# Output stores of the last stage split over two DMA queues, even token tiles on ScalarE's and odd ones on SyncE's

## The reference

```python
logits = jnp.einsum('ed,btd->bte', gate_w, x)
scores = jax.nn.sigmoid(logits) + gate_b
weights, indices = jax.lax.top_k(scores, TOP_K)          # TOP_K = 4
weights = weights / weights.sum(-1, keepdims=True)
...
h3 = jax.nn.silu(h1 * h2)                                # per expert
experts_out = jnp.einsum('btec,ecd->bted', h3, w2_routed)
routed_out = jnp.einsum('bted,bte->btd', experts_out, router_probs)
return shared_out + routed_out
...
x = x + jnp.tanh(g_ffn[0]) * _L0_ffn_ref(_layernorm(x), ...)
```

## Time and profile before

| what | us |
|---|---|
| median of 3 runs | 913.25 (912.56 to 913.78) |
| the profiled execution | 911.14 |
| its span, first to last instruction | 909.4 |
| TensorE busy | 787.8 (87%) |
| GpSimd busy | 505.7 (56%) |
| VectorE busy | 453.4 (50%) |
| ScalarE busy | 285.7 (31%) |

### The profile page before, as it was taken

The page is one execution under the profiler, slowest core; times in us unless marked ns, Lnnn a source line. Parts: engine busy times, 40 slices in busy tenths (PEclk is TensorE's granted clock), DMA queues, the critical chain, the costliest instruction groups (busy, mean ns, idle before and its releaser), DMA issues.

```text
span 909.4 us, 16740 instructions
## 1 busy us (share of the span) xinstructions
PE 787.8 (87%) x4484; PEld 684.9 (75%) x4485; DVE 453.4 (50%) x916; ACT 285.7 (31%) x572; POOL 505.7 (56%) x361
## 2 busy tenths in 40 slices
PE   4455869888995979999999999998899999999991
PEld 3233667666774869998998998997789998888891
DVE  5886868897867553334333333333233333333331
ACT  1426537456351112222222222222132232222220
POOL 1744075083278670250786751776870587978782
PEclk9776969998998979999999999999899999999997
DMA  7448176189133433352566454464552469779999
GB/s 256 152 134 287 47 286 240 56 318 388 38 153 111 183 111 101 93 166 70 153 188 179 147 150 127 142 196 130 162 188 81 126 191 197 164 164 210 215 188 266
DMA packets 68858, 153.54 MB, mean 169 GB/s; under 512 B 6720, under 2 KB 8768, under 8 KB 68832
## 3 DMA queue, kind: packets, MB, share of 16 engines
q0 software_dynamic: 24400, 70.86, 30.0%
q1 hardware_dynamic: 33920, 61.13, 20.7%
q10 hardware_dynamic: 10512, 21.23, 6.4%
HBM read 85.43 MB, written 67.76 MB: 168 GB/s over the span
## 4 chain that ended last, share of the span: by engine, by line
PE 59%; DVE 12%; POOL 12%; DMA 4%; ACT 4%; issue 4%; ACTq 2%; POOLq 0%; SPq 0%; DVEq 0%
PE bank L600 32%; PE bank L617 14%; POOL ring_lo L436 4%; DMA wa<-in_ctx_dram 3%; PE bank L1013 3%; PE bank L608 3%; POOL acc L570 3%; PE bank L625 2%; PE bank L710 2%; POOL dispatched L474 2%; DVE amax L1454 2%; POOL ring_hi L434 2%; PE bank L728 1%; ACTq L1163 1%; DVE xa L1447 1%
## 5 line engine op out<-in xcount | busy, mean ns | idle before, releaser
L600 PE MATMUL bank<-ring_hi,xr_hi 128*128 x632 | 170.4, 351 | 16.3 <-DVE xr_lo L1917 16.3
L600 PE MATMUL bank<-ring_lo,xr_hi 128*128 x632 | 156.2, 329 | 0.0
L600 PE MATMUL bank<-ring_hi,xr_lo 128*128 x632 | 155.8, 328 | 0.0
L434 POOL CAST ring_hi<-raw 128x1408 fp32r<-128x1408 f32 x34 | 47.0, 1382 | 169.6 <-PE bank L600 158.6
L600 PEld LDWEIGHTS bank<-ring_hi,xr_hi 128*128 128x128 f32 x632 | 107.1, 193 | 40.3 <-issue 40.2
L1069 ACT ACTIVATE ht_hi<-bank 128x384 fp32r<-128x384 f32 x95 | 46.7, 492 | 281.1 <-PE bank L608 281.1
L1926 DVE TENSOR_TENSOR ht_lo<-bank,ht_hi 128x384 fp32r<-128x384 f32 x79 | 44.1, 558 | 170.7 <-ACT ht_hi L1069 170.6
L617 PE MATMUL bank<-ring_hi,ht_hi 112*128 (+3 forms) x285 | 120.4, 422 | 3.6 <-DVE ht_lo L1926 1.3
L600 PEld LDWEIGHTS bank<-ring_lo,xr_hi 128*128 128x128 f32 x632 | 113.6, 192 | 0.0
L600 PEld LDWEIGHTS bank<-ring_hi,xr_lo 128*128 128x128 f32 x632 | 113.5, 192 | 0.0
L570 POOL DMA_INDIRECT acc<-expert_out,out_row x64 | 99.6, 1556 | 24.7 <-issue 24.7
(11 more groups left out here) (181 smaller groups left out, 1295.9 us busy)
## 6 DMA issues: line engine op xcount, KB each, us to landing
raw<-in_L_ffn_w_routed_dram POOLq DMA_DIRECT2D x32, 704.0 KB, 4.9
x_in<-dispatched SPq DMA_DIRECT2D x79, 264.0 KB, 2.9
expert_out<-zero_rows ACTq DMA_DIRECT2D x9, 2304.0 KB, 19.2
expert_out<-y_out SPq DMA_DIRECT2D x79, 256.0 KB, 2.9
raw<-in_L_ffn_w_routed_dram POOLq DMA_DIRECT2D x16, 448.0 KB
dispatched<-zero_rows SPq DMA_DIRECT2D x1, 4224.0 KB, 27.6
acc<-in_x_dram SPq DMA_DIRECT2D x4, 1024.0 KB, 11.4
wa<-in_fside_BxS2xS_dram SPq DMA_DIRECT2D x4, 1024.0 KB, 6.7
```

Of the source, the lines that this page charges most:

```text
L434: g.tensor_copy(hi, raw13[:, :, m, :]).then_inc(s[rounded], 1)
L600: last = mm(outs[m], half[:, c * P:(c + 1) * P], ring13(w, slot_at, c, m), start=(c == 0 and half is x_hi and w is ring13_hi), stop=(c == ...
```

## The change

The 16 output stores are divided. ScalarE's queue gets those of the even token tiles, behind its last `tile_step`; SyncE keeps those of the odd ones. Each still waits for the four gathers of its own token tile. SyncE's two waits for the stores to `expert_out` stand behind its output stores now, and not ahead of them. SyncE's last wait, for all 16 output stores, is unchanged.

```diff
                 sp.wait_ge(s["d_y_e"], t + 1)
                 store_tile(t, t % 2)
 
+            for t in range(1, TT, 2):
+                sp.wait_ge(tile_gathered[t], 16 * TOPK)
+                sp.dma_start(out_rows[t], acc_tile(t)).then_inc(s["out_stored"], 16)
             for k in range(2):
                 sp.wait_ge(y_stored[k], 16 * ((TILES + 1 - k) // 2))
-            for t in range(TT):
-                sp.wait_ge(tile_gathered[t], 16 * TOPK)
-                sp.dma_start(out_rows[t], acc_tile(t)).then_inc(s["out_stored"], 16)
             sp.wait_ge(s["out_stored"], 16 * TT)
...
             for t in range(3 + 2 * len(range(3, TILES - 2, 2)), TILES + 1):
                 tile_step(t, t % 2)
+            for t in range(0, TT, 2):
+                act.wait_ge(tile_gathered[t], 16 * TOPK)
+                act.dma_start(out_rows[t], acc_tile(t)).then_inc(s["out_stored"], 16)
```

## The result

| kernel | median us (runs) | ratio to before, 95% interval |
|---|---|---|
| before | 912.86 (6, 909.95 to 913.78) | |
| with the change | 908.19 (6, 907.13 to 911.21) | 0.9959 (0.994 to 0.9978) |

The kernel is faster by 0.41%, some 3.7 us, with an interval from 2.0 to 5.5 us. I had forecast 0.24% and 911.05 us, with a range down to 910.3.

What follows compares the result with a forecast made beforehand. The prediction took DMA work with one hole to bound the last 20 us. Gains of 1.70 us (hole) and 0.5 us (rate), less 0 for late gathers, made 2.2 us: 913.25 to 911.05 us, range 910.3 to 912.7.

Steps and rivals of the forecast that it cites:

- What bounds the end: Last 20 us: DMA work sets the end, with one hole while SyncE waits for the last expert store.
- first term: Stretches from 895 us: earlier output stores fill the hole in DMA work, gaining 1.70 us (1.0 to 1.75).
- second term: Output stores at the end: two queues write at 411 GB/s instead of 382, gaining 0.5 us (0 to 0.78).
- third term: Last gathers sharing engines with stores: tile 15's lands later, at about 901, costing 0 us (0 to 1.7).
- rivals of late: Tile 15's gather lands at 904 to 905, leaving a new hole; gain 0 to 1.3 us; chance 0.18.
- dearer gathers: Gathers mixed with stores cost more per packet, so DMA work grows and the time is over 915 us; chance 0.06.
- The level and the range: Median 913.25 us less 2.2 gives 911.05; lower end 910.3 allows 0.4 us for run-to-run movement, upper end 912.7.

Runs made afterwards that it cites:

- SyncE alone: Against the kernel before, all 16 output stores stay on SyncE's queue but no longer wait for the expert_out stores; ratio 0.9968.
- ScalarE's queue alone: All 16 output stores issued early from ScalarE's queue in order, none on SyncE's; ratio to before 0.9972.
- seven early stores: Against the changed kernel, SyncE issues the stores of tiles 0 to 6 between its last expert stores; 907.46 and 907.66 us, ratios to before 0.9942 and 0.995.
- split and late: Against the changed kernel, both queues wait for all expert_out stores before their eight output stores; ratio to before 0.9999.
- evens first: Against the kernel before, one queue behind the same wait, even tiles stored first and odd ones after; ratio 0.9989.
- two more gathers: The kernel before with two gathers added behind the last one, into a dead buffer of GpSimd; ratio 1.0006.
- SyncE's half late: Stores split, ScalarE's eight early as in the change, SyncE's eight behind the expert_out wait as before; ratio to before 0.9962.

## Why the prediction was wrong where it was

**What bounds the end** was right: DMA work with a hole in it, and every run that kept the hole kept the tail.

**The first term**, 1.70 us for the hole, was right in its mechanism. The hole is gone in the changed kernel. With SyncE alone and no hole the tails are 1.1 to 1.55 us shorter, which already has a little of the rate in it, so the term was sized somewhat high, if one trace can tell.

**The second term** had about the right size, by luck, and the wrong cause. I had put the 411 GB/s of the earlier trace rows down to two queues at work. The run with two queues behind the hole gave 379, the one with ScalarE's queue alone 404. The rule of the Trainium skill, page "DMA: Bandwidth & Descriptors", section "Rules for kernel authors", that more issuing engines don't help bandwidth, stands in these runs; it was my reading of the row that failed. But the second term of 0 that I drew from it doesn't hold either, because the rate went up to 406 by another way: an earlier start among gathers. From 901 on 2.7 MB moved at 406 instead of 382, in 6.6 us instead of 7.0, which is 0.4 us. I had also carried over an issue of 0.33 to 0.65 us from one queue; with two it took about 1.2, which cost nothing here.

**The third term**, 0, was right. The last gather's landing, the two lines of it in the changed kernel:

```profile
L570 POOL DMA_INDIRECT acc<-expert_out,out_row x1: 1554/1554/1554, 892.3 to 892.3; - x1
...
DMA to landing us min/median/max: 9.5/9.5/9.5
```

It landed 9.5 us after its start where I had put 10.7, at 901.8, and later stores kept the engines full behind it. The rivals of late and of dearer gathers did not come true. The DMA share from the same point before the last expert store to the end was 0.96 x 18.9 = 18.1 us against 18.4.

**A term was missing.** 1.7 and 0.4 make 2.1, the tails say 1.4 to 1.9. The difference points to the last row of the changed kernel's stretches above: 12 GB/s from 908 to 909. Had all engines ended together, the bytes from 907 to 908, at 246 GB/s, would have been the last, at about 907.6; one or a few ran on for another microsecond. In the earlier trace rows the stores still ran at 195 GB/s in that row, half of it full, and the span closed 0.4 us behind it. The version with seven early stores has such an end too, 33 and then 10 GB/s in its last two full microseconds, and the second trace of before has none. An estimate from such rows puts a number on it: from the moment at which all bytes would be through at the full rate to the end of the span it is 0.9 us in the five traces whose stores began behind the hole and without the added DMA (before twice, split and late, evens first, two more gathers), and 1.7, 1.7 and 2.2 in the three of the changed kernel. So the term is 0.8 to 1.3 us, and the prediction had put nothing in its place. With it the sum comes to 0.8 to 1.3 us and the tails say 1.4 to 1.9, so it closes to about half a microsecond, which is as near as these traces tell. A share of 0.03 of 16 engines is one engine at work for half of the microsecond. That engines which come out of mixed work don't end together, and that the last store pays for it, is an inference from the rows; no run took it away.

**The level and the range** are what missed. The step that failed is the sentence that the median "has itself moved by 0.6 us either way", with the 0.4 us that the range allowed for it. That was read from three runs between 912.56 and 913.78. Single runs of the same kernel later ranged from 907.4 to 917.6, two outliers over 1000 aside, with medians of 911.45 to 913.39 in six groups of runs, and medians of the changed kernel of 908.19, 910.56 and 911.18. Two of these lie within my range and one does not. The forecast gain of 2.2 us lies within the interval of the first ratio (2.0 to 5.5), and near the 2.4 us of the three together. A range for one median of six runs should have had some 2 us more on either side for the spread ahead of 340 us. One number at hand hinted at it: the profiled execution, 911.14, stood 2.1 us below the median. That the first comparison came out at 3.7 us and not near 2 was chance, in part at least, so that no term of the sum accounts for it.

## What to carry to other kernels

Look at the share of the DMA engines, microsecond by microsecond, behind the last computing instruction: a hole there is what an early issue can win first. The rest here was small beside it: some 0.4 us from the rate, and 0.8 to 1.3 us lost again at the end. Any queue that has ready work during the other one's wait fills it, so that moving a wait behind the stores was worth as much here, within the scatter, as a second queue, and stores issued still earlier, in SyncE's idle time while gathers ran, were worth more than both, though the DMA share there was near 1 already. When a gain is a few microseconds and the first stages spread by seven, compare tails counted from a fixed event in several traces, and take the spread of the level into the range.

## What the runs showed of the hardware

The rate of plain stores of 256 KB went with what ran when they began: 379 to 385 GB/s in the six traces that began them on empty or nearly empty engines (behind the hole), and 402 to 407 in those that began them well among gathers, on one queue or two. Between the two stand SyncE alone, early, with one or two microseconds of overlap (403, falling to 382 at the end), and SyncE's late half beside the last of ScalarE's early one (393). The DMA share reads 1.03 to 1.04 in the first and 1.05 to 1.06 in those among gathers.

An issue took longer where other DMAs filled the engines: 1.25 us in the median on SyncE and 1.17 on ScalarE in the changed kernel, and 1.19 on both with two late queues, against 0.64 before. A second store queue isn't needed for it. With SyncE's half late, the first line below, ScalarE issued its eight stores among gathers, before SyncE's first one at 898.96, and they took 1.26. The other two lines are of the changed kernel. Nobody waited for the longer issues there:

```profile
L1398 ACTq DMA_DIRECT2D out_dram<-acc x8: 345/1262/1622, 887.7 to 896.0; - x8
```
```profile
L348 SPq DMA_DIRECT2D out_dram<-acc x8: 1176/1254/1736, 894.8 to 904.6; - x8
```
```profile
L1398 ACTq DMA_DIRECT2D out_dram<-acc x8: 345/1168/1781, 890.0 to 898.5; - x8
```
